# A gated block with mLSTM attention and ternary weights: the first running maxima in four row groups, the last steps reordered, and three weight pieces scaled on GpSimd

## What is computed

```
LN(x)    = layernorm over the last axis, no weights
q        = LN(x);  k = v = ctx_1024                       # [16, 256, 512], 8 heads of 64
ig, fg   = concat(q, k, v) @ igate + bias, concat(q, k, v) @ fgate + bias      # [16, 256, 8]
cs       = cumsum(log_sigmoid(fg)) along the tokens
log_D    = where(lower triangle, cs[i] - cs[j] + ig[j], -inf);  m = max over j of log_D
C        = (q k^T / 8) * exp(log_D - m)
h        = C / (max(|sum_j C|, exp(-m)) + 1e-6) @ v,  then h * rsqrt(mean(h^2) + 1e-6) per head
x        = x + tanh(g_xattn) * h
# feed-forward with weights rounded to -1, 0, 1 and tokens rounded to 8 bits
wq(w)    = clip(round(w * s), -1, 1) / s,  s = 1 / max(mean|w|, 1e-5)
aq(y)    = clip(round(y * t), -128, 127) / t,  t = 127 / max|y| per token
g, u     = aq(LN(x)) @ wq(w_gate)^T, aq(LN(x)) @ wq(w_up)^T                    # 512 -> 2048
x        = x + tanh(g_ffn) * aq(relu(g)^2 * u) @ wq(w_down)^T                  # 2048 -> 512
```

## Time and profile before

| | us |
|---|---|
| median of 3 runs (612.22 to 612.51) | 612.44 |
| profiled execution | 614.58 |
| its span in the trace | 612.9 |
| PE busy | 569.6 (93%) |
| DVE busy | 526.9 (86%) |
| ACT busy | 452.7 (74%) |
| POOL busy | 125.9 (21%) |

### The profile page before, as it was taken

How to read it: one execution, slowest core, us unless ns; L and a number is a source line. 1 busy time by engine, 2 the same in 40 slices (tenths; PEclk the granted TensorE clock), 3 DMA queues, 4 the chain that set the end, 5 groups by cost and what they waited for, 6 DMA issues and landing times.

```text
span 612.9 us, 18356 instructions
## 1 busy us (share of the span) xinstructions
PE 569.6 (93%) x6526; PEld 342.2 (56%) x6605; DVE 526.9 (86%) x1148; ACT 452.7 (74%) x923; POOL 125.9 (21%) x281
## 2 busy tenths in 40 slices
PE   7967578999999999999999999999999999999896
PEld 4744343656556565656556565656565565656443
DVE  4497989898989999898989899898989899897964
ACT  5578868868686868778687868778686968687662
POOL 2236151112121203012121212022121212021100
PEclk9589869999999999999999999999999999999999
DMA  8937305050230506050321405050412305030000
GB/s 319 383 132 250 130 2 190 3 182 28 94 115 18 189 0 206 0 189 17 134 72 39 167 17 189 0 194 13 164 42 76 130 18 190 2 105 1 22 33 34
DMA packets 44113, 62.68 MB, mean 102 GB/s; under 512 B 1848, under 2 KB 25648, under 8 KB 44080
## 3 DMA queue, kind: packets, MB, share of 16 engines
q1 hardware_dynamic: 44080, 62.24, 28.9%
HBM read 53.72 MB, written 8.51 MB: 102 GB/s over the span
## 4 chain that ended last, share of the span: by engine, by line
PE 80%; DVE 10%; issue 5%; ACT 2%; POOL 2%; DMA 1%; SPq 0%; DVEq 0%; ACTq 0%; POOLq 0%
PE yb L1181 17%; PE gb L1155 16%; PE ub L1155 16%; PE tp L1202 8%; PE ab L1189 7%; PE ab L1169 4%; PE tp L1229 3%; PE ab L1212 2%; PE ab L1190 2%; POOL stage L439 1%; PE ab L1263 1%; DVE asum L763 1%; DVE stage L785 1%; DVE dmat L898 1%; DVE stage L770 1%
## 5 line engine op out<-in xcount | busy, mean ns | idle before, releaser
L1155 PE MATMUL ub<-wuT,xqT 128*128 128x512 bf16 x498 | 129.4, 381 | 2.5 <-DVE stage L785 1.7
L1155 PE MATMUL gb<-wgT,xqT 128*128 128x512 bf16 x479 | 127.1, 382 | 4.9 <-issue 4.1
L1181 PE MATMUL yb<-wdT,stage 128*128 128x512 bf16 x482 | 114.3, 379 | 6.6 <-ACT stage L549 3.5
L535 ACT ACTIVATE relu<-gb 128x512 f32<-128x512 f32 x128 | 75.4, 589 | 48.8 <-PE gb L1155 48.4
L785 DVE TENSOR_TENSOR stage<-relu,ub 128x512 f32<-128x512 f32 x128 | 86.8, 678 | 15.9 <-ACT relu L537 15.9
L898 DVE SCALAR_TENSOR_TENSOR dmat<-ab,dmat 128x384 f32<-128x384 f32 x128 | 65.1, 549 | 25.8 <-POOL dmat L447 16.2
L1155 PEld LDWEIGHTS ub<-wuT,xqT 128*128 128x128 bf16 x512 | 49.6, 98 | 64.3 <-DVE stage L785 5.0
L537 ACT ACTIVATE relu<-relu 128x512 f32<-128x512 f32 x128 | 80.8, 631 | 4.1
L1181 PEld LDWEIGHTS yb<-wdT,stage 128*128 128x128 bf16 x512 | 47.0, 98 | 51.7 <-issue 4.3
L1155 PEld LDWEIGHTS gb<-wgT,xqT 128*128 128x128 bf16 x512 | 46.1, 101 | 45.4 <-issue 1.3
L447 POOL TENSOR_SCALAR_AFFINE_SELECT dmat<-dmat 128x256 f32<-128x256 f32 x128 | 55.6, 463 | 66.1 <-ACT dmat L595 50.6
(11 more groups left out here) (124 smaller groups left out, 886.6 us busy)
## 6 DMA issues: line engine op xcount, KB each, us to landing
dmat<-max_rows SPq DMA_DIRECT2D x15, 1024.0 KB, 5.0
values<-in_ctx_v SPq DMA_DIRECT2D x16, 520.0 KB, 7.6
xs<-in_x SPq DMA_DIRECT2D x16, 512.0 KB, 5.8
cT<-in_ctx_t SPq DMA_DIRECT2D x16, 512.0 KB, 6.8
out<-stage SPq DMA_DIRECT2D x32, 256.0 KB, 2.0
stage<-in_w_gate SPq DMA_DIRECT2D x4, 1024.0 KB, 12.2
stage<-in_w_up SPq DMA_DIRECT2D x4, 1024.0 KB, 13.1
stage<-in_w_down SPq DMA_DIRECT2D x4, 1024.0 KB, 5.4
```

Source lines behind the costliest of these rows:

```text
L535: nc.scalar.activation(relu[:, c % 2, :], gb[c % 2][:, :], ACT.Relu).then_inc(g_free, 1)
L1155: last = nc.tensor.matmul(bank[c % 2][:, :], xqT[par][:, t, d, :], w[:, d, c * CH:(c + 1) * CH], start=(d == 0), stop=(d == KD - 1))
L1181: done = nc.tensor.matmul(yb[:, :], hqT[:, c, :], wdT[:, c, :], start=(c == 0), stop=(c == KF - 1))
```

## The change

Four things are changed.

- **First maxima.** A new buffer a_groups holds a of batch 0 four times, in columns 0 to 7 of four groups of 32, the rest zero. `first_cumulative` writes it on DVE (one instruction more), `first_a_rows` transposes 128 columns in place of 8, and `first_running_max` scans 128 rows in place of 8. `spread_first_max` takes pair p from rows 32p to 32p + 7, so that the four pairs stand in four row groups of the array; its eight matmuls come in a row, ahead of all scores. `keep_warm` counts in the prologue go from 3, 1, 2, 1 to 5, 2, 4, 8 in batch 0 and from 6, 6, 20 to 2, 6, 4, 8, 14 around batch 1.
- **Up pieces.** Pieces 1, 2 and 3 of w_up are scaled by GpSimd in quarters. DVE no longer scales them and rounds all three (`round_weight`); ACT no longer takes the sign of piece 1.
- **Order in the prologue and in step 0.** On ACT the sum over w_gate's piece 2 moves ahead of the second copy of heads, sign_weight(0, 0) behind the w_up sums, sign_weight(0, 1) behind `tokens`. On DVE `gates_in(1)` moves ahead of `head_squares(0)`. In step 0 `hidden(0, 0, 0)` moves ahead of `round_weight(2)`, and `weight_scale(2)` from behind `normaliser` to behind `log_forget`. On PE `weight_total(2)` moves from between the heads to behind `gate_products`, with chunk(0, 1, 0) behind it.
- **The last two steps.** In step 14 ACT copies ab0 (`hidden_cols(14, 0)`) before `tokens_rstd`. In step 15 `quantise_high(14, 1)`, `hidden_transposes(14, 1)` and both `hidden_cols(14, 1)` move ahead by one or two chunks.

The loop's twelve steps and step 13 keep their order.

```diff
-        mrow = sb("mrow", [NH, S], F32)
+        mrows = sb("mrows", [P, S], F32)
+        mrow = mrows[0:NH, :]
...
-        pick = hq[0][0:NH, :].bitcast(F32)
+        pick = hq[0][:, 0:2 * 2 * P].bitcast(F32).rearrange("p (r c) -> p r c", r=2)
+        GROUP = P // NP
+        a_groups = sb("a_groups", [P, T, NP, GROUP], F32)
...
-            nc.gpsimd.memset(zeros8[:, :], 0.0).then_inc(consts, 1)
+            nc.gpsimd.memset(zeros[:, :], 0.0).then_inc(consts, 1)
+            nc.gpsimd.memset(a_groups[:, :, :, :], 0.0).then_inc(consts, 1)
...
+            for g in range(NP):
+                if g > 0:
+                    gp.wait_ge(pick_step, g)
+                nc.gpsimd.affine_select(out=pick[:, :, :], in_=pick[:, :, :], compare_op=ALU.not_equal, fill=1.0,
+                                        base=-(GROUP + 2) * g, pattern=[[-1, 2], [0, P]], channel_multiplier=1).then_inc(pick_step, 1)
...
+            scale_weight(1, 1)
             scale_weight(0, 3)
             masks(1, 0)
+            scale_weight(1, 2)
+            scale_weight(1, 3)
...
@@ -651,25 +662,25 @@
             for p in range(NP):
                 first_exponentials(p)
             heads(0, 0)
+            magnitudes(0, 2, 1)
+            heads(0, 1)
             exp_minus_max(0, 0)
-            magnitudes(0, 2, 1)
-            for p in range(1, NP):
-                heads(0, p)
+            heads(0, 2)
+            heads(0, 3)
             squares(0)
             for t in range(T):
                 columns(1, qT[1], t)
             magnitudes(1, 0, 2)
-            sign_weight(0, 0)
             forget_gate(1)
             head_rms(0)
             magnitudes(1, 2, 3)
             magnitudes(1, 3, 4)
+            sign_weight(0, 0)
             tokens_rstd(0)
-            sign_weight(0, 1)
             sign_weight(1, 0)
             quantise_second(0)
             tokens(0, 0)
-            sign_weight(1, 1)
+            sign_weight(0, 1)
...
+                if n is None:
+                    quantise_high(b - 1, 1)
...
-                if prev:
+                if n is None:
+                    hidden_cols(b - 1, 1)
+                elif prev:
                     quantise_high(b - 1, 1)
...
-                if prev:
+                if prev and n is not None:
                     hidden_cols(b - 1, 1)
...
+                if m is None:
+                    hidden_cols(b, 0)
                 if n is not None:
                     tokens_rstd(n)
-                hidden_cols(b, 0)
+                if m is not None:
+                    hidden_cols(b, 0)
...
             def round_weight(i):
 
-                dve.wait_ge(w_scaled_here, i + 1)
+                dve.wait_ge(w_scaled[1], i)
                 nc.vector.tensor_scalar(ternary_piece(1, i), by_rows(weight_piece(1, i)), MAGIC32, -1.0,
                                         ALU.subtract, ALU.max).then_inc(w_low, 1)
-                dve.wait_ge(w_low, i - 1)
+                dve.wait_ge(w_low, i)
...
+            def first_cumulative():
+                dve.wait_ge(tp_full, FULL * (gate_use(0, CUMSUM) + 1))
+                cs = tp[:, 0:T * NH].rearrange("p (t g) -> p t g", t=T)
+                nc.vector.tensor_tensor(a_groups[:, :, :, 0:NH], gates[:, :, None, 0:NH].to_broadcast([P, T, NP, NH]),
+                                        cs[:, :, None, :].to_broadcast([P, T, NP, NH]), ALU.subtract).then_inc(group_step, 1)
+                nc.vector.tensor_copy(csum[:, :, :], cs).then_inc(gate_step, 1)
+                nc.vector.tensor_tensor(a[0][:, :, :], gates[:, :, 0:NH], cs, ALU.subtract).then_inc(tp_free, 1)
+
+            def first_running_max():
+
+                dve.wait_ge(tp_full, FULL * (gate_use(0, A_ROWS) + 1))
+                nc.vector.tensor_tensor_scan(mrows[:, :], tp[:, 0:S], zeros[:, :], LOWEST,
+                                             ALU.max, ALU.add).then_inc(tp_free, 1)
...
-            cumulative(0, 0)
+            dve.wait_ge(consts, 11)
+            first_cumulative()
             dve.wait_ge(q_ready, Q_K)
             attention_moments(1)
-            running_max(0, 0)
+            first_running_max()
...
             magnitudes(1, 1)
+            gates_in(1)
             head_squares(0)
-            gates_in(1)
...
-            scale_weight(1, 1)
+            round_weight(1)
...
+                hidden(b, 0, 0)
                 if not prev:
-                    scale_weight(1, 2)
                     round_weight(2)
-                hidden(b, 0, 0)
...
                 if not prev:
-                    scale_weight(1, 3)
                     round_weight(3)
...
+                if n is None:
+                    hidden_cols(b - 1, 1)
...
+                hidden_scale(b, 0, par)
+                quantise_low(b, 0)
+                if n is not None:
+                    head_squares(n)
+                if m is not None:
+                    gates_in(m)
+                if n is not None:
+                    mean_squares(n)
+                if m is not None:
+                    log_forget(m)
                 if not prev:
                     weight_scale(2)
                     dve.wait_ge(winv_step, WINV[2])
                     nc.vector.scalar_tensor_tensor(wprod[:, 2:3], wmean[:, 2:3], 1.0 / 127.0, tanhs[:, 1:2],
                                                    ALU.mult, ALU.mult).then_inc(winv_step, 1)
-                hidden_scale(b, 0, par)
-                quantise_low(b, 0)
-                if n is not None:
-                    head_squares(n)
-                if m is not None:
-                    gates_in(m)
-                if n is not None:
-                    mean_squares(n)
-                if m is not None:
-                    log_forget(m)
...
                             pe.wait_ge(w_ready[0], c + 1)
-                        elif c < 2:
-                            pe.wait_ge(w_high, c + 1)
+                        elif c == 0:
+                            pe.wait_ge(w_high, 1)
                         else:
-                            pe.wait_ge(w_ready[1], c - 1)
+                            pe.wait_ge(w_ready[1], c)
...
-            def spread_max(p):
-
-                if p == 0:
-                    pe.wait_ge(tp_free, gate_use(0, A_ROWS) + 1)
+            def first_a_rows():
+                pe.wait_ge(tp_free, gate_use(0, CUMSUM) + 1)
+                pe.wait_ge(group_step, 1)
+                for t in range(T):
+                    last = nc.tensor.transpose(tp[:, t * P:(t + 1) * P], a_groups[:, t, :, :].rearrange("p g w -> p (g w)"), ident[:, :])
+                last.then_inc(tp_full, FULL)
+
+            def spread_first_max():
+
+                pe.wait_ge(pick_step, NP)
+                pe.wait_ge(tp_free, gate_use(0, A_ROWS) + 1)
                 for e in range(2):
-                    hd = 2 * p + e
-                    done = nc.tensor.matmul(spread_rows[p][:, e * S:(e + 1) * S], pick[:, hd * P:(hd + 1) * P], mrow[:, :],
-                                            start=True, stop=True)
-                done.then_inc(rows_spread, 1)
+                    for p in range(NP):
+                        rows = slice(GROUP * p, GROUP * p + NH)
+                        done = nc.tensor.matmul(spread_rows[p][:, e * S:(e + 1) * S], pick[rows, e, :], mrows[rows, :],
+                                                start=True, stop=True)
+                        if e == 1:
+                            done.then_inc(rows_spread, 1)
...
-            keep_warm(3, yb)
+            keep_warm(5, yb)
             cumulative_sum(0)
-            keep_warm(1, yb)
-            a_rows(0, 0)
             keep_warm(2, yb)
-            spread_max(0)
-            spread_max(1)
+            first_a_rows()
+            keep_warm(4, yb)
+            spread_first_max()
             scores(0, 0, 0)
             scores(0, 1, 0)
-            spread_max(2)
-            spread_max(3)
             max_columns(0)
-            keep_warm(1, yb)
+            keep_warm(8, yb)
...
+            q_columns(1, 1)
+            keep_warm(2, yb)
             weight_total(0)
-            q_columns(1, 1)
             gate_products(1, 1, 0, T * 2 * KD)
             keep_warm(6, ub[1])
             cumulative_sum(1)
+            keep_warm(4, ub[1])
             a_rows(1, 1)
-            keep_warm(6, ub[1])
+            keep_warm(8, ub[1])
             weight_total(1)
             max_columns(1)
-            keep_warm(20, ub[1])
+            keep_warm(14, ub[1])
             token_columns(0)
...
+                if n is None:
+                    hidden_transposes(b - 1, 1)
                 chunk(b, 0, 3, par)
                 if n is not None:
                     heads_out(n, 2, npar)
-                if prev:
+                if prev and n is not None:
                     hidden_transposes(b - 1, 1)
-                else:
-                    weight_total(2)
...
-                if m is not None:
+                if not prev:
+                    weight_total(2)
```

(10 more changed lines are left out.)

29 lines of the change are left out of this document (15 added, 14 removed).

## The result

The changed kernel takes 626.72 us (median of 4 runs, 625.93 to 627.45) where the kernel before takes 612.48 beside it (612.22 to 612.61): 1.0233 of its time, 95% interval 1.0215 to 1.0251. The forecast was 610.5 us, 607.8 to 613.3. The profiled execution took 627.18 us, its span is 625.5 us.

The account below looks back on a forecast made before the run. PE was taken to bound the loop, and a chain through DVE, ACT and GpSimd, with PE at low clock, the beginning. Start 0.8 plus ending 1.2 gave 2.0 us: 612.44 becomes 610.5 us, range 607.8 to 613.3.

Parts of the forecast that it names:

- First maxima, row groups: Prologue, batch 0: four pairs' products side by side by 14.9 us, last copy of heads 6.1 us earlier; in turn, chance 0.06.
- The up pieces: Prologue, w_up pieces moved to GpSimd: of 5.9 us gained, 2.3 are left when DVE reaches hidden(0, 0, 1).
- w_down's scale: Step 0, scale moved later: GpSimd starts w_down 0.95 us later than before, residual ends at 90.4; the start gives 0.8 us.
- the lost cover: Step 0: DVE formerly reached the second statistics only at 91.2 us, after the residual's 89.52; now GpSimd is late next.
- The ending: Last two steps: earlier copies spare PE waits, third relu_square of the last tile 1.2 us earlier (bounds 0 and 2).
- The 2.0 of the prediction's last section: Sign expected in the profile after: third relu_square of the last tile starts 2.0 us earlier than before.
- the change doesn't touch its order, so nothing is won or lost there.: Loop, 105 to 540 us: PE busy 426.6 of 435.0 us, its order unchanged, so gain or loss put at nothing.
- I carry every difference over to it unchanged: Whole kernel: differences summed against the profiled 614.58 us apply equally to the median, 2.14 us lower.
- The terms of the start: Before the loop: first maxima 6.1 us earlier, 2.3 left after the up pieces, 0.8 us left after w_down's scale.
- slower: Whole kernel: outcome slower than the kernel before, given chance 0.13; faster by over 0.2% had 0.63, same 0.24.
- GpSimd or the clock: Prologue rivals: GpSimd becomes the bound, 615.6 us, chance 0.09; clock falls as before, 614.1 us, chance 0.05.

## Why the prediction was wrong

Up to the loop it held, against the profiled execution that it was summed on. The rows of after for it (PE and ACT at the first maxima; GpSimd; DVE's hidden(0, 0, 1) and second statistics):

```profile
13.90 0.41 PE L1313 MATMUL gb<-mrows,hq 8*128 8x256 f32 x2
13.95 0.38 PE L1313 MATMUL ub<-mrows,hq 8*128 8x256 f32 x2
...
14.75 0.63 ACT L586 ACTIVATE dmat<-gb,a 128x128 f32<-128x128 f32 x2 [1.50 <-PE ub L1313]
```

```profile
42.05 3.84 POOL L447 TENSOR_SCALAR stage<-stage,winv 128x512 f32<-128x512 f32 x4 [9.59 <-DVE wprod L1056]
...
47.07 6.78 POOL L447 TENSOR_SCALAR stage<-stage,winv 128x512 f32<-128x512 f32 x8
...
81.19 6.79 POOL L447 TENSOR_SCALAR stage<-stage,winv 128x512 f32<-128x512 f32 x8 [16.71 <-DVE winv L776]
...
88.18 1.26 POOL L462 TENSOR_TENSOR x<-ysq,xs 128x512 f32<-128x512 f32 x1
```
```profile
64.95 0.67 DVE L803 TENSOR_TENSOR stage<-relu,ub 128x512 f32<-128x512 f32 x1
...
89.48 0.69 DVE L983 BATCH_NORM_STATS2 st<-x 128x6 f32<-128x512 f32 x1 [3.25 <-POOL x L462]
```

- *First maxima, row groups.* Right. The eight spread products lie side by side, the first exponentials start at 14.75, the clock is 1.00 to 28.2. The last copy of heads ends at 25.26 (forecast 25.9), winv of w_gate starts at 26.82 (27.95).
- *The up pieces.* Right: third w_gate piece 42.05 (41.9), the next two pieces 6.78 us (2.7 and 4.2 forecast), hidden(0, 0, 1) 64.95 (65.05).
- *w_down's scale.* Right in mechanism: GpSimd starts at 81.2 (81.6), the residual ends at 89.44 (90.4), DVE's second statistics wait for it and start at 89.48. PE's step 1 is 1.1 us earlier than in the trace of before (0.8). I named the lost cover and did not draw the conclusion: it is the one reordering that was found to cost, 2.2 us in the trace.
- *The ending.* Right mechanism, 1.0 us for 1.2: the third relu_square of the last tile starts at 610.07, and 597.42 + 13.67 would be 611.09. (The 2.0 of the prediction's last section is this 1.2 and the start's 0.8.) What it left out is that the clock can fall in the ending's waits, which takes 1.5 us in some executions.
- *"the change doesn't touch its order, so nothing is won or lost there."* This is the step that failed: the term for the loop was put at nothing, and it is +14.8 us in the trace. The order is the same; the code's place isn't. I counted the added keep-warm matmuls in the prologue, at 0.22 us each in PE's waits, and not as 28 instructions ahead of a loop. None of my rivals was of this kind, so the range was too narrow by its premise and not by a term. The trace of before had the hint: no instruction transfer on queue 8 from 170 to 500 us, so the loop runs on held code.
- *"I carry every difference over to it unchanged"* failed too, for some 1.5 us. The terms of the start were taken against an execution in which the clock was low for 13.7 us from 14.5 us on, and one of them was just to end that. Without long branches (fewer matmuls) the change gives 0.66 us of medians (612.79 and 612.13; 0.4 to 1.8 by the interval), not 2.0. The traces split it into the ending's 1.0, where the clock doesn't take it back, and a start 0.6 us later than in an execution of the old prologue at the better clock (172.39 for 171.76 at tile 5); these are single executions, so the split is rough.

The chance on "slower" was 0.13, all of it on GpSimd or the clock. With the long branches taken out, the measured 612.13 us lies inside the range, 1.6 us above the forecast; the sum of 2.0 us didn't come true.

## What to carry to other kernels

Count the instructions ahead of and inside a hardware loop for the engine that bounds it: if its code fills nearly all the blocks that the engine was seen to hold (seven here), any insertion ahead of it, however cheap, can cost a refetch in each pass. The signs are an "issue" wait of some microseconds at the first line of the loop, and instruction transfers inside the loop's stretch; removing a few instructions, or adding up to the next whole block, tests it. Before costing a change against a profiled execution, ask whether that execution is a typical one, above all if the change mends just what made it slow. And where a sum says "the cover is gone, this engine is late next", try the order without that move first.

## What the runs showed of the hardware

- A branch back of PE with transfers of its code behind it took 5.7 to 7.7 us, one without 0.21 to 0.25; the period of tiles grew by 7.1 to 7.7 us for one in the trace of after.
- With the loop 128 instructions past its place in the kernel before all five branches missed in the profiled execution; 16 and 30 past it, one or two did, and between four executions of one program (16 more) the time ranged from 612.96 to 628.46 us.
- TensorE's clock fell to 0.50 with the holes of after (from 173.1 to 179.9 us, hole from 170.3 to 176.1; from 319.9 to 323.3 us, hole from 314.7 to 320.0). What this adds to their price isn't separated.
- 110 matmuls of one column took 27 ns each, with a hole of 2.65 us after the first three; of 30 matmuls of 128 columns in the same place, there is one of 2.5 us after the first three as well.
- With the new ending, 3 of 8 traces have the clock at 0.50 for 3.4 us behind the last `rhm`, and 11.6 to 11.7 us from it to the end for 10.0 to 10.1; none of 5 with the old ending does.
- Executions of one program differed by up to 3 us (612.02 to 614.99, 19 runs of before). In the traces 1.7 us of such a difference go with how long the clock was low from 14 to 28 us.
